# Window attention of an eight-stage network: six stack buffers, three output buffers and another order of SyncE's transfers

## What is computed

```
x = x + L0_conv(gn(x))         # window attention, both shifts 0 and 2: touched
x = x + L1_conv(gn(x))
t = to_tokens(x)
t = t + L2_attn(ln(t)); t = t + L2_ffn(ln(t)); t = t + L3_attn(ln(t)); t = t + L3_ffn(ln(t))
```

```
q, k, v = split(einsum('bchw,oc->bohw', roll(x, -s)[half], wq))
attn = softmax(q k^T * scale)            # 8 heads of 8 channels, windows of 128 tokens
o = attn v + depthwise_conv(v)           # the convolution is done in an earlier stage
out[half] += roll(o, s)
```

## Time and profile before

| | |
|---|---|
| time, three runs | 4033.07, 4028.87, 4033.74 us (median 4033.07) |
| profiled execution | span 4026.0 us from its first to its last instruction; the record has no separate time for what lies around it, and the median of the runs is 7.1 us more |
| the stage of the change | from 300 us (first memset) to 813 us, 513 us |
| busy over the span | PE 85%, DVE 62%, ACT 48%, POOL 21% |
| busy in the 513 us | PE 390.7, DVE 347.9, ACT 318.7, POOL 177.4 us |
| granted TensorE clock in the 513 us | mean 0.79 (1.00 is 2.4 GHz, 0.50 is 1.2 GHz) |

### The profile page before, as it was taken

How to read it: one execution, slowest core, us unless ns; L and a number is a source line. 1 busy time by engine, 2 the same in 40 slices (tenths; PEclk the granted TensorE clock), 3 DMA queues, 4 the chain that set the end, 5 groups by cost and what they waited for, 6 DMA issues and landing times. The chain is left out here.

```text
span 4026.0 us, 66483 instructions
## 1 busy us (share of the span) xinstructions
PE 3440.5 (85%) x24463; PEld 1530.3 (38%) x24463; DVE 2489.7 (62%) x4082; ACT 1927.2 (48%) x2321; POOL 860.5 (21%) x866
## 2 busy tenths in 40 slices
PE   6997887647599999999999998789878479999999
PEld 4664555424322222222222221633567334444444
DVE  3227767465489999998999995344486323333333
ACT  1214667512147777777777777334323223233322
POOL 0001333300000000000000000034200245555555
PEclk9997778778779999999999999789989589999999
DMA  4444555400500000000000000044101122222221
GB/s 144 125 126 103 115 118 119 88 1 2 180 18 16 21 21 21 22 20 21 15 26 21 16 21 6 17 138 150 53 0 43 33 81 85 84 87 85 84 84 47
DMA packets 137544, 247.17 MB, mean 61 GB/s; under 512 B 34808, under 2 KB 47264, under 8 KB 136800
## 3 DMA queue, kind: packets, MB, share of 16 engines
q1 hardware_dynamic: 137312, 243.98, 21.8%
HBM read 171.55 MB, written 56.62 MB: 57 GB/s over the span
## 5 line engine op out<-in xcount | busy, mean ns | idle before, releaser
L1073 DVE TENSOR_REDUCE mxv<-mx_ps 128x1 f32<-128x512 f32 x2048 | 1276.9, 683 | 88.8 <-PE mx_ps L932 70.6
L1048 ACT ACTIVATE PT<-st_ps 128x1024 f32<-128x1024 f32 x1024 | 997.1, 1022 | 297.3 <-PE st_ps L945 297.1
L932 PE MATMUL mx_ps<-KS,QS 24*128 24x512 f16 x2048 | 613.3, 394 | 114.0 <-DVE mxv L1073 96.6
L1921 DVE TENSOR_TENSOR u<-h_ps,s 128x512 f32<-128x512 f32 x352 | 243.5, 692 | 541.6 <-ACT s L1899 494.6
L959 PE MATMUL o_ps<-PT,VA 128*32 128x512 f32 x4096 | 550.0, 609 | 0.5 <-ACT PT L1048 0.5
L1951 POOL TENSOR_TENSOR hg<-u,gb 128x512 f32<-128x512 f32 x352 | 450.9, 1283 | 394.1 <-DVE u L1921 297.4
L1899 ACT ACTIVATE s<-h_ps 128x512 f32<-128x512 f32 x352 | 210.2, 597 | 587.3 <-PE h_ps L1875 587.3
L1883 PE MATMUL y_ps<-hg,m_w 128*128 128x512 f32 x704 | 361.4, 597 | 55.2 <-POOL hg L1951 55.1
L945 PE MATMUL st_ps<-QS,KS 26*128 26x512 f16 x2048 | 400.4, 387 | 9.2 <-ACT TX L1038 8.5
L667 DVE TENSOR_REDUCE mxv<-mx_ps 128x4 f32<-128x512 f32 x512 | 319.7, 683 | 118.3 <-PE mx_ps L542 113.8
L945 PEld LDWEIGHTS st_ps<-QS,KS 26*128 26x128 f16 x2048 | 96.5, 91 | 558.2 <-issue 479.7
(11 more groups left out here) (228 smaller groups left out, 4173.1 us busy)
## 6 DMA issues: line engine op xcount, KB each, us to landing
gb<-g SPq DMA_DIRECT2D x64, 512.0 KB, 3.7
gb<-g SPq DMA_DIRECT2D x16, 2048.0 KB
QK<-qk SPq DMA_DIRECT2D x128, 192.0 KB
qk<-hl SPq DMA_DIRECT2D x80, 256.0 KB, 3.3
RB<-d SPq DMA_DIRECT2D x48, 256.0 KB, 3.5
qk<-hl SPq DMA_DIRECT2D x64, 128.0 KB, 3.2
v<-vs SPq DMA_DIRECT2D x32, 256.0 KB
VS<-v SPq DMA_DIRECT2D x32, 256.0 KB, 3.1
```

Source lines behind the costliest of these rows:

```text
L932: nc.tensor.matmul(mx_ps[:, use % 3, :], rows(QS, g // 2, j, STACK)[:, t * C:(t + 1) * C], rows(KS, g // 2, j, STACK)[:, half * HALF:(half ...
L1048: nc.scalar.activation(PT[:, n % 2, 2 * a:2 * a + 2], st_ps[:, a], ACT.Exp, scale=1.0 / SHIFT ** 2).then_inc(st_free[a], 1)
L1073: nc.vector.tensor_reduce(mxv[:, g % 2, j, t, half:half + 1], mx_ps[:, slot], AX.X, ALU.max).then_inc(mx_free, 1)
```

## The change

- Six stack buffers in place of four. Group g = 4i + u uses stack g mod 6, and `load_qk` fetches five groups ahead (five groups are fetched before the loop). SP no longer puts `load_qk` at the head of a group but after the rows.
- The constant rows are written per stack by a memset of 2048 f32 (two f16 of 32768 in one word) that covers Q and K, six of them, where it was one of 8192 f16 over K alone; SP waits for each.
- Three output buffers OR in place of two; the semaphores of denominators and regrouping are one per u.
- `spread` is cut in two: `store_inverse` (store) stays at the end of u = 3 (half 0) and of u = 1 of the next image (half 1); the load of RB comes later, at u = 0 of the next image (half 0) and u = 2 (half 1), behind `load_rows`.
- `load_den` moves ahead of `load_rows`; `regroup` stays behind, after `load_qk`.
- POOL's program is as before but for the semaphores' names.

```diff
...
+MAX_UNITS = 2.0 ** 113 * (1 + 30720 / 2.0 ** 23)
...
+    STACKS, OUTS = 6, 3
...
-        QK = chip.buf(ctx, "QK", [C, U, 2, S, N], F16)
+        QK = chip.buf(ctx, "QK", [C, STACKS, 2, S, N], F16)
...
-        OR = chip.buf(ctx, "OR", [C, 2, S, N])
+        OR = chip.buf(ctx, "OR", [C, OUTS, S, N])
...
-                def spread(i, h):
+                def store_inverse(i, h):
 
                     count = i * 2 + (h + 2)
                     sp.wait_ge(x_done, count)
                     sp.wait_ge(inverted, count)
                     sp.dma_start(d_scr[i, h].rearrange("a p n -> p a n"), RD[:]).then_inc(rd_stored, 16)
+
+                def spread(i, h):
+
                     sp.wait_ge(rd_stored, i * 32 + (16 * h + 32))
...
+                for g in range(5):
+                    sp.wait_ge(ones_set, g + 1)
+                    load_qk(g // U, g % U)
+                    if g < 2:
+                        load_v(0, g)
                 sp.wait_ge(mx_free, 20 + 1 + 3)
-                load_rows(0)
+                load_rows(0, 0)
...
                         if i or u:
                             sp.wait_ge(st_ready[1], i * STEPS + 4 * u)
-                        if u == 0 and kind != "first":
-                            load_qk(i, 3)
-                        if u and kind != "last":
-                            load_qk(i + 1, u - 1)
+                        if group(i, u):
+                            load_den(i - (u == 0), (u + 3) % U)
                         if kind != "last" or u < 3:
                             sp.wait_ge(mx_free, i * PER + (LEAD + MX[kind]["turn", u, TURNS[u][-1]] + 1 + 3))
-                            load_rows((u + 1) % 4)
-                        if u:
-                            load_den(i, u - 1)
-                            regroup(i, u - 1)
-                        elif kind != "first":
-                            load_den(i - 1, 3)
-                            regroup(i - 1, 3)
+                            load_rows(i + (u == 3), (u + 1) % U)
+                        if u == 0 and kind != "first":
+                            spread(i - 1, 0)
+                        if u == 2 and kind != "first":
+                            spread(i - 1, 1)
+                        if group(i, u) + 5 < B * U:
+                            load_qk(i + (u + 5) // U, (u + 5) % U)
+                        if group(i, u):
+                            regroup(i - (u == 0), (u + 3) % U)
                         if kind != "last" or u < 1:
                             sp.wait_ge(va_done, i * U + (u + 2))
                             load_v(i + (u + 3) // 4, (u + 3) % 4)
                         if u == 3:
-                            spread(i, 0)
+                            store_inverse(i, 0)
                         if u == 1 and kind != "first":
-                            spread(i - 1, 1)
+                            store_inverse(i - 1, 1)
...
-                    if n % 4 == 0:
-                        act.wait_ge(regrouped[u % 2], i * 256 + (u // 2 * 128 + 128))
-                        act.wait_ge(den_loaded[u % 2], i * 32 + (u // 2 * 16 + 16))
...
+                    if n % 4 == 0 and g >= OUTS:
+                        before = g - OUTS
+                        act.wait_ge(regrouped[before % U], 128 * (before // U + 1))
+                        act.wait_ge(den_loaded[before % U], 16 * (before // U + 1))
...
-                nc.vector.memset(KS, MAX_UNIT).then_inc(ones_set, 1)
+                for k in range(STACKS):
+                    nc.vector.memset(KS[:, k].rearrange("p s n -> p (s n)").bitcast(F32), MAX_UNITS).then_inc(ones_set, 1)
...
```

More of the change, by code:

```diff
@@ L408, in mx_uses, with group, stack @@
         return numbered(uses)
+    def group(i, u):
+        return i * U + u
+    def stack(i, u):
+        return group(i, u) % STACKS
     MX = {kind: mx_uses(kind) for kind in ("first", "mid", "last")}
@@ L433, in window_attention @@
         o_ps = chip.psum(ctx, "o_ps", [C, HALF])
-        qk_loaded = [chip.sem("qk_loaded") for _ in range(U)]
-        rows_loaded, v_loaded, den_loaded, rb_loaded, regrouped, st_ready, st_free = ([chip.sem(s) for _ in range(2)] for s in (
-            "rows_loaded", "v_loaded", "den_loaded", "rb_loaded", "regrouped", "st_ready", "st_free"))
+        qk_loaded = [chip.sem("qk_loaded") for _ in range(STACKS)]
+        den_loaded, regrouped = ([chip.sem(s) for _ in range(U)] for s in ("den_loaded", "regrouped"))
+        rows_loaded, v_loaded, rb_loaded, st_ready, st_free = ([chip.sem(s) for _ in range(2)] for s in (
+            "rows_loaded", "v_loaded", "rb_loaded", "st_ready", "st_free"))
         (filled, ones_set, mx_ready, mx_free, split, va_done, pv_done, o_free, inverted, rd_stored,
@@ L466, in load_den @@
                     sp.wait_ge(o_free, i * STEPS + (4 * u + 5))
-                    sp.dma_start(DEN[:, u // 2, u % 2], OR[D:C:32, u % 2].rearrange("j s n -> j (s n)")).then_inc(den_loaded[u % 2], 16)
+                    o = group(i, u) % OUTS
+                    sp.dma_start(DEN[:, u // 2, u % 2], OR[D:C:32, o].rearrange("j s n -> j (s n)")).then_inc(den_loaded[u], 16)
                 def regroup(i, u):
@@ L534, in _, with rows, max_scores @@
             def _(pe):
-                def rows(buf, u, s, j, count):
-                    return buf[32 * j:32 * j + count, u, s]
-                def max_scores(u, n, j, use):
+                def rows(buf, k, s, j, count):
+                    return buf[32 * j:32 * j + count, k, s]
+                def max_scores(k, n, j, use):
                     for w in range(4):
@@ L542, in max_scores @@
                         mm = nc.tensor.matmul(mx_ps[:, use % 3, w * C:(w + 1) * C],
-                                              rows(QS, u, n // 2 % 2, j, STACK)[:, at],
-                                              rows(KS, u, n // 2 % 2, j, STACK)[:, at], start=True, stop=True)
+                                              rows(QS, k, n // 2 % 2, j, STACK)[:, at],
+                                              rows(KS, k, n // 2 % 2, j, STACK)[:, at], start=True, stop=True)
                     mm.then_inc(mx_ready, 1)
@@ L549, in turn, with scores @@
                                         ident[:]).then_inc(mx_ready, 1)
-                def scores(n, a):
-                    u, s = n // 4, n // 2 % 2
+                def scores(i, n, a):
+                    k, s = stack(i, n // 4), n // 2 % 2
                     if a == 1:
-                        fill_array(nc, st_ps[:, a, 1], ident, KS[:, u, s, 0:HALF])
+                        fill_array(nc, st_ps[:, a, 1], ident, KS[:, k, s, 0:HALF])
                     for w in range(4):
@@ L557, in scores @@
                         for e in range(2):
-                            mm = nc.tensor.matmul(st_ps[:, a, e, w * C:(w + 1) * C], rows(KS, u, s, 2 * a + e, ROWS)[:, at],
-                                                  rows(QS, u, s, 2 * a + e, ROWS)[:, at], start=True, stop=True)
+                            mm = nc.tensor.matmul(st_ps[:, a, e, w * C:(w + 1) * C], rows(KS, k, s, 2 * a + e, ROWS)[:, at],
+                                                  rows(QS, k, s, 2 * a + e, ROWS)[:, at], start=True, stop=True)
                     mm.then_inc(st_ready[a], 1)
@@ L596, in image @@
                             if with_max:
-                                pe.wait_ge(qk_loaded[(u + 2) % 4], i * 64 + (64 if u < 2 else 128))
+                                g = group(i, u + 2)
+                                pe.wait_ge(qk_loaded[g % STACKS], 64 * (g // STACKS + 1))
                         def ahead(j):
@@ L601, in ahead @@
                                 pe.wait_ge(mx_free, i * PER + (use + 1))
-                                max_scores((u + 2) % 4, n, j, use)
+                                max_scores(stack(i, u + 2), n, j, use)
                         for a, pair in enumerate(PAIRS):
@@ L607, in image @@
                                 warm_up(nc, st_ps[:, a, 0], identf, X)
-                            scores(n, a)
+                            scores(i, n, a)
                             for j in pair:
@@ L674, in invert @@
                 def invert(i, h):
-                    for s in den_loaded:
-                        v.wait_ge(s, i * 32 + (h * 16 + 32))
+                    for s in den_loaded[2 * h:2 * h + 2]:
+                        v.wait_ge(s, i * 16 + 16)
                     v.wait_ge(rd_stored, i * 32 + (h * 16 + 16))
@@ L741, in finish @@
                     for part in range(2):
-                        pool.wait_ge(regrouped[part], i * 256 + (128 * h + 256))
+                        pool.wait_ge(regrouped[2 * h + part], i * 128 + 128)
                     pool.wait_ge(rb_loaded[h], i * 32 + 32)
```

29 lines of the change are left out of this document (13 added, 16 removed).

## The result

Median of seven runs 4051.58 us (4042.75 to 4063.28) against 4033.24 (4028.87 to 4039.67) for the kernel before, again seven: ratio 1.0044, 95% interval 1.0029 to 1.0058. The change makes the kernel slower, by some 18 us (12 to 23), where 48 were forecast. The profiled execution took 4046.21 us with a span of 4044.4, so 1.8 us lie around a span, not the 7.1 of the prediction: with the same 1.8 us the profiled execution of the kernel before (span 4026.0) took 4027.8, some 5 us under its median. The spans differ by 18.4 us.

What follows compares the result with a forecast made beforehand. PE's wait for the rows of maxima (48.7 us) and slow clock came on top of DVE's reductions, the floor. Terms +41.7 + 2.9 + 2.5 + 0.7 = +48 us gave 4081 us against 4033.07, range 4043 to 4105.

Steps and rivals of the forecast that it cites:

- the stall on rows goes: PE's wait for the rows of maxima, sent ahead of the bulk, set to zero: -48.7 us if nothing replaced it.
- RB behind the rows: RB's later load delays POOL's finish and the split behind it, so PE idles 7.2 us at the next turn.
- T + 2.65 and 7.2 and 8.5 + 0.1: Chain from turn T: RB issued after 2.65 us, finish starts 7.2 later, finish and split 8.5, next turn 0.1.
- 13 even intervals: Turn to turn in groups u = 0 and u = 2, where POOL has a finish: 18.4 us each.
- Rival A: The finish does not hold up the turn, 25 groups of 11.2 us: 3949 us, faster; chance 0.08.
- B: Bulk behind one group's rows still moving at the next turn, 3 us in 12 odd intervals: 4117 us; chance 0.04.
- C: RB lands 4.8 us after issue instead of 7.1, nothing being ahead of it: 4051 us; chance 0.05.
- D: The stall at the turn does not lower PE's clock, 13 x 2.9 us less: 4043 us; chance 0.04.
- 12 odd intervals: Turn to turn in the groups without a finish: 11.2 us plus 2.9 for slow clock, 14.1 each.
- start: Stage start: six memsets take 10.4 us where one took 6.9, and DVE gives PE its credits later: +0.7 us.
- the clock: After each late turn PE works 10.2 us at clock 0.50, costing 2.9 us, all in the odd interval.
- Priced at nothing: Parts given no effect on time, among them fetching stacks five groups ahead and the third output buffer.

Runs made afterwards that it cites:

- e3: Kernel before with only the load of RB moved behind the rows of u = 0 and u = 2: 4052.82 us, ratio 1.0046.
- e1: Changed kernel with POOL splitting the maxima before it does the finish, RB still late: 3980.28 us, ratio 0.9875.
- e2: Changed kernel with RB loaded at the head of the even groups and the inverses stored ahead of regrouping, POOL's order kept: 3979.0 us, ratio 0.9876.
- e4: Changed kernel with the load of RB also behind the four stack loads: 4091.27 us, ratio 1.0155.
- e5: Changed kernel with RB loaded at the head of the groups and the maxima split before the finish: 3962.27 us, ratio 0.9827.
- e8: Changed kernel with RB at the head, maxima split before the finish, and two output buffers in place of three: 3958.79 us, ratio 0.9836.
- e7: Kernel before with RB's load behind the rows and the maxima split before the finish: 3981.19 us, ratio 0.9884.
- e11: Changed kernel with RB at the head, split before finish, two output buffers, and four stacks fetched three groups ahead: 4026.12 us, ratio 0.9989.

## Why the prediction was right and wrong

**Right: the stall on rows goes** (0.2 us left over the stage). **Right: RB behind the rows is what decides.** T + 2.65 and 7.2 and 8.5 + 0.1 were the steps; measured 2.6, 7.0 and 8.4 + 0.06. I had 13 even intervals of 18.4 us; they were 17.8 to 19.2, 18.3 on average. 13 waits were forecast at 7 us each, some 90; they were 85.7. e3 shows that this one step makes the slowdown, e1 and e2 that each link of the chain is needed for it. Rival A (the gain arrives) fell because the chain did not fit; B (rows late as well) by the wait of 0.2 us; C (RB lands sooner) by 7.0 us: the 3.5 of the earlier trace rows does not hold for this transfer, and neither does the fit for the GpSimd path in the Trainium skill (DMA: Bandwidth & Descriptors, Anatomy of one DMA), which would have each of the two land 2.6 us after its issue, an estimate. That the median, 4051.58, is C's 4051 is chance: RB landed no sooner. D (no drop of the clock) fell too, for the clock is at 0.50 for 145 of the 388.5 us, though its 4043 is nearer to the result than my 4081.

**Wrong: the size, by a factor of 2.6.** Against the terms of the sum:

| term | forecast | measured |
|---|---|---|
| 13 even intervals | 239.2 | 237.7 |
| 12 odd intervals | 169.2 | 150.7 |
| 25 groups against 366.7 | +41.7 | +21.8 |
| start (T(1,0) from the first memset: 90.0 before, 86.0 after) | +0.7 | -4.0 |
| T(7,1) to POOL's last large addition (53.7 before, 57.9 after) | +5.4 | +4.2 |
| earlier and later stages | 0 | -3.6 |
| sum, spans | +48 | +18.4 |

The odd intervals make 18.4 of the 29.4 us by which the terms are off. The step that failed is their price, *the clock*: "work at 0.50 for 10.2 us after the late turn costs 2.9 us", on top of a full group of 11.2, 14.1 us in all. The full group rests on the sentence on the stall, that everything else waits, "so nothing covers it". An odd interval took 12.6. Both parts were too large, by about 0.8 us each.

*The slow work.* The 10.2 us came from the kernel before, where I had taken the fall into the idle time off the total and treated the rest as a fixed price that follows every stall. A spell is a stretch at 0.50. Summing (1 - clock)/0.5 over half-microsecond stretches of the trace, and within them PE's busy time:

| kernel | stalls | PE's idle time per stall | at 0.50 per stall | of it work |
|---|---|---|---|---|
| before | 12 | 4.1 | 11.9 | 9.2 |
| changed | 13 | 6.6 | 11.8 | 7.2 |
| e3 | 12 | 6.9 | 12.5 | 7.3 |
| e4 | 11 | 11.7 | 14.0 | 4.1 |

(The twelfth spell of the kernel before follows a shorter dip of PE at 586 us. The row of e4 stops at 760 us.) On average a spell is 12 to 14 us in all four kernels. Most begin in the idle time, and a longer idle time uses more of them up: work at 0.50 falls as idling grows. That was put on record before e4 as one of two readings, and e4 decides for it: 3.0 to 4.2 us of slow work in 12 of its 13 spells. Single spells differ widely, 3.4 to 23.9 us in the kernel before and 6.8 to 20.5 in the changed one, so 9.2 against 7.2 alone would not show it. In the stretches of the changed kernel around its first stall, one of the short ones, the clock is at 0.50 before PE resumes at 403.20, and back within 4 us:

```profile
400.00:402.00 2.00, 0.00 (x0) 0.00 (x0) 0.00 (x0) 0.00 (x0) 2.00 (x1) 0.55 0.50 129
...
406.00:408.00 2.00, 1.92 (x41) 0.95 (x33) 1.71 (x3) 1.58 (x3) 0.00 (x0) 0.75 0.73 178
```

against over 9 us in the kernel before.

*The group itself.* Three odd intervals of the changed kernel with little, much and nothing but slow clock (columns as in the earlier trace rows):

```profile
403.20:414.86 11.66, 11.11 (x262) 7.22 (x263) 9.88 (x17) 8.90 (x11) 2.13 (x5) 0.84 0.54 123
524.41:538.63 14.22, 14.10 (x262) 9.16 (x263) 9.88 (x17) 9.29 (x11) 2.14 (x5) 0.57 0.45 101
649.87:665.17 15.30, 15.30 (x261) 9.93 (x262) 9.83 (x16) 9.32 (x11) 2.15 (x5) 0.50 0.42 94
```

A straight line through all twelve odd intervals, length against PE's work at 0.50 within them, is 10.4 us plus 0.31 us for each us of slow work (e3: 10.3 and 0.31; e4: 10.6 and 0.28). So the 29% of the prediction was right, and 6.85 us of slow work cost 2.1 us. What was wrong is the 11.2 under it. DVE's reductions alone, one even and one odd interval (us, DVE busy and, touched by the stretch, how many; then clock, DMA share, GB/s), first in the changed kernel, then in the kernel before:

```profile
385.11:403.20 18.09, 11.26 (x18) 0.92 0.52 121
403.20:414.86 11.66, 8.80 (x15) 0.84 0.54 123
```
```profile
390.05:407.24 17.19, 10.07 (x16) 0.77 0.66 143
407.24:419.82 12.58, 10.08 (x17) 0.78 0.39 78
```

In each of the 13 even intervals of the changed kernel DVE gets through 18 reductions, and in each odd one through 14, where PE gives it 16 in both; e3 and e4 are the same, and in e5 and e8, without the stall, it is 16 and 16. While the turn waits, DVE works off two score tiles that would otherwise fall into the odd interval. So the stall is covered in part: 10.08 - 8.80 = 1.3 us of DVE's work. An odd interval of e5 or e8 without slow clock takes 11.1 to 12.7 us, most often 11.59; less 1.3 that is 10.3, an estimate, against the 10.4 of the line. This is read from traces; no run changed it by itself.

The second miss is the start: six memsets of 2048 words were priced where there are six of 1024. 4.7 us too much, most of it from a misread slice (six of 2048 were 10.4 us by the forecast, six of 1024 are 5.5); the instruction list of the changed kernel says 128x1024. Of the 3.6 us of other stages 0.9 lie before the stage's first memset and 2.7 behind POOL's last large addition, where the change touches nothing.

Priced at nothing and right: the third output buffer (e8). Priced at nothing and right only as long as RB is late: the stacks fetched far ahead (e7 against e1: nothing; e11 against e8: 67 us, with the limits said at e11).

## What to carry to other kernels

When a transfer is moved back so that another can go first, follow the moved one to its consumer and on through everything that is queued behind that consumer: the chain's parts (2.65 + 7.2 + 8.5 us) all stood in the trace of before, and the engine at its end was 21% busy. A change can be right in its parts and lose by one line: the six stacks and the new order gain 1.7% once RB leaves at the head of the group and the small urgent instruction goes ahead of the long one on POOL (e5). Two edits of order in the kernel before already gain 1.2% (e7). And do not add the price of the slow clock to a stall as a constant: look at how much of the slow spell the stall itself covers, and at what the other engines catch up in it (two of 16 reductions here).

## What was not expected of the hardware

- A slow spell of TensorE's clock lasted 12 to 14 us on average, whether PE's stall was of 4 us or of 12 (table above). In e1 and e5 spells also came with idle places of no more than 3.5 us, though not with each of them, and one spell of e1, at 489.67 us, had no idle place of 0.9 us near it.
- From the issue of RB's two transfers of 256 KB to the finish's start 6.8 us pass with nothing else to move (issued at 819.73, finish at 826.55, changed kernel), and while they alone move only half of the DMA engines' time is used (columns as in the earlier trace rows):

```profile
821.00:823.00 2.00, 0.00 (x0) 0.00 (x0) 0.00 (x0) 0.00 (x0) 1.94 (x2) 0.50 0.51 125
```

  The Trainium skill (DMA: Bandwidth & Descriptors, Rules for kernel authors) says that a leading zero-stride broadcast of c copies confines a DMA to at most c engines of the 16; RB's source is such a broadcast of 8. The share of 0.51 agrees; a transfer of another shape was not tried.
- The constants as f32 words: 1024 in 0.91 us, where 8192 f16 took 6.88. Four of 0.91 fill what took 6.88. The Trainium skill (VectorE: DVE Perf Modes, Zero memsets can be issued as uint32) gives one cycle per element whatever the type and recommends the wider type for zero. The trace agrees, with 0.89 ns per element as f32 and 0.84 as f16; here it works for a constant that is not zero, two f16 packed in one f32.
